# Four graph layers in one kernel: the attention layer's low halves accumulated into the high halves' columns

## The reference, cut to what matters

```python
x = (meta_x @ W).reshape(N, HEADS, DIM)              # HEADS = 4, DIM = 64
a_src = jnp.sum(x * att_src, axis=-1)
a_dst = jnp.sum(x * att_dst, axis=-1)
logits = jax.nn.leaky_relu(a_src[src] + a_dst[dst], 0.2)
ex = jnp.exp(logits - seg_max[dst])
alpha = ex / (seg_sum[dst] + 1e-16)                  # sums over the edges into dst
out = segment_sum(x[src] * alpha, dst).mean(heads) + bias
```

## Time and profile before

| | |
|---|---|
| runs | 1197.7, 1198.29, 1210.78 us, median 1198.29 us |
| profiled execution | 1197.28 us, span 1195.4 us |
| mean granted clock of PE | 0.968 |
| attention, first mask product to last | 772.57 to 1187.08 us |
| after the last product | 8.32 us |

### The profile page before, as it was taken

The page is one execution under the profiler, slowest core; times in us unless marked ns, Lnnn a source line. Parts: engine busy times, 40 slices in busy tenths (PEclk is TensorE's granted clock), DMA queues, the critical chain, the costliest instruction groups (busy, mean ns, idle before and its releaser), DMA issues.

```text
span 1195.4 us, 38826 instructions
## 1 busy us (share of the span) xinstructions
PE 1082.5 (91%) x15999; PEld 997.2 (83%) x15999; DVE 863.9 (72%) x2311; ACT 628.7 (53%) x1172; POOL 59.6 (5%) x106
## 2 busy tenths in 40 slices
PE   4877777779999999999998999599999999999997
PEld 3766666669999999999973999489989988998996
DVE  5999999975444444444562544789999999999997
ACT  2777777730000000000111402579989999998997
POOL 1000000001111111111000011000000000000000
PEclk7899999989999999999999799699999999999999
DMA  5555555510000000000000000000000000000010
GB/s 80 69 78 77 72 74 73 71 39 3 2 3 2 3 2 3 2 2 3 2 2 1 2 2 2 15 12 13 24 12 24 13 24 13 24 13 20 16 29 14
DMA packets 135931, 28.04 MB, mean 23 GB/s; under 512 B 132609, under 2 KB 133093, under 8 KB 135778
## 3 DMA queue, kind: packets, MB, share of 16 engines
q1 hardware_dynamic: 132816, 25.25, 12.9%
q10 hardware_dynamic: 2962, 0.58, 0.3%
HBM read 24.97 MB, written 0.85 MB: 22 GB/s over the span
## 4 chain that ended last, share of the span: by engine, by line
PE 63%; DVE 12%; ACT 3%; issue 2%; ACTq 0%; POOL 0%; DVEq 0%
PE bank L2018 33%; PE bank L2141 13%; PE bank L2137 6%; DVE Mr L1587 4%; PE bank L1955 3%; PE bank L2207 2%; PE bank L1947 2%; ACT Mr L966 1%; DVE F L1487 1%; PE bank L1982 1%; PE bank L1939 1%; ACT F L907 1%; PE bank L2040 1%; DVE Mr L1597 1%; DVE FN L1489 0%
## 5 line engine op out<-in xcount | busy, mean ns | idle before, releaser
L2018 PE MATMUL bank<-GH,C 128*128 128x128 f16 x7100 | 397.7, 219 | 0.0
L2018 PEld LDWEIGHTS bank<-GH,C 128*128 128x128 f16 x7100 | 396.9, 98 | 0.1
L2141 PE MATMUL bank<-F,Mr 128*128 128x260 f16 (+1 forms) x2538 | 321.2, 261 | 10.0 <-DVE Mr L1587 8.7
L2141 PEld LDWEIGHTS bank<-F,Mr 128*128 128x128 f16 x2538 | 213.2, 98 | 33.7 <-DVE Mr L1587 11.0
L1587 DVE TENSOR_TENSOR Mr<-Mr,C 128x640 f16<-128x640 f16 x461 | 207.6, 485 | 25.4 <-ACT Mr L966 24.3
L814 ACT ACTIVATE plo<-bank 128x256 f32<-128x256 f32 (+1 forms) x84 | 30.1, 360 | 364.3 <-PE bank L2018 346.0
L2137 PE MATMUL bank<-FN,C 128*128 128x130 f16 x1945 | 187.3, 220 | 0.0
L1234 DVE TENSOR_TENSOR S<-bank,plo 128x256 f32<-128x256 f32 (+1 forms) x84 | 33.2, 395 | 212.9 <-ACT plo L814 212.8
L1810 PE MATMUL bank<-ohk,ohp 128*128 128x100 f16 (+3 forms) x1452 | 115.9, 216 | 69.6 <-ACT C L756 35.1
L966 ACT ACTIVATE Mr<-cold,eaT 128x640 f16<-128x640 f32 x231 | 172.4, 819 | 8.1 <-PE bank L2141 7.7
L966 ACT ACTIVATE Mr<-eaT 128x640 f16<-128x640 f32 x230 | 171.7, 818 | 7.3 <-PE bank L2141 7.0
(11 more groups left out here) (271 smaller groups left out, 984.4 us busy)
## 6 DMA issues: line engine op xcount, KB each, us to landing
raw<-in_edges_dram SPq DMA_DIRECT2D x237, 68.0 KB, 2.5
cold<-minus_dram SPq DMA_DIRECT2D x10, 320.0 KB, 3.3
eaT<-minus_dram SPq DMA_DIRECT2D x9, 320.0 KB, 3.5
xs<-in_x_dram SPq DMA_DIRECT2D x1, 800.0 KB, 4.4
out_dram<-xs SPq DMA_DIRECT2D x4, 160.0 KB
raw<-in_edges_dram ACTq DMA_DIRECT2D x5, 68.0 KB, 3.2
dsts<-in_dst_dram SPq DMA_DIRECT2D x1, 240.0 KB
dsts<-in_dst_dram ACTq DMA_DIRECT2D x1, 180.0 KB
```

Source lines behind the costliest of these rows:

```text
L2018: last = pe.matmul(bank[:, b, jj * 2 * D:(jj + 1) * 2 * D], C[:, t, (t0 + jj) * P:(t0 + jj + 1) * P], GH[:, par, t, :], start=t == 0 and j ...
L2141: return pe.matmul(bank[:, k, a_:z_], Mr[:, mi % RB, j * P:(j + 1) * P], F[:, t, a_:z_], start=start, stop=t == T - 1)
```

## The change

- `FS` = 16: both copies of the features are scaled by 16 in place of 2048 (`E2`), the high part is the plain float16 rounding, the low part the unscaled difference (a TENSOR_TENSOR subtraction in place of a SCALAR_TENSOR_TENSOR at L1487).
- High and low parts go into the same columns of PSUM. `plain`, `masked` and the `Nr` products each become two products with the same weights, one of the high part and one of the low part, accumulated into the same columns: 260 columns become 2 x 130 (two runs of 65 each), 130 become 2 x 65.
- What is taken out of PSUM is therefore 65 columns a copy in place of 130 (`take`, `evicted`, `tile_in`), `r1` is half as wide, and the addition of the low parts (L1502, L1609) is gone. `q` is gone, `r1` takes its place.
- Bounds: `WIDEST` 12 in place of 16; a second maximum over the weights with the bound `HEAVIEST` = 3.5 on the squared column norm; two small operations on DVE for it in the first hop.
- SP waits for its store of `minus_row` before it looks at the flag, not behind it.

```diff
@@ attention, ACT
-    act.activation(pairs_of(t0)[:, :, 0, :], Vx[gi % 2]..., ACT.Copy, scale=1.0 / LO).then_inc(s_fhi, 1)
+    act.activation(pairs_of(t0)[:, :, 0, :], Vx[gi % 2]..., ACT.Copy).then_inc(s_fhi, 1)
...
-    act.activation(r1[:, j], bank[:, BANKS[b][j], 0:2 * S1], ACT.Identity, scale=ex[:, 1, h, t:t + 1]).then_inc(s_c2, 1)
+    act.activation(r1[:, j], bank[:, BANKS[b][j], 0:S1], ACT.Identity, scale=ex[:, 1, h, t:t + 1]).then_inc(s_c2, 1)
@@ weights(3), DVE
-    c.add(v.tensor_reduce(wmax[:], bank[0:1, 7, 0:GS + H], AX, ALU.max))
+    c.add(v.tensor_reduce(wmax[:, 0:1], bank[0:1, 7, 0:GS + H], AX, ALU.max))
+    c.add(v.tensor_reduce(wmax[:, 1:2], bank[0:1, 7, 0:H * D], AX, ALU.max))
+    c.here()
+    c.add(v.scalar_tensor_tensor(wmax[:, 0:1], wmax[:, 1:2], 900.0 / HEAVIEST, wmax[:, 0:1], ALU.mult, ALU.max))
@@ low_f, evicted, post, DVE
-    c.add(v.scalar_tensor_tensor(pairs_of(t0)[:, :, 1, :], pairs_of(t0)[:, :, 0, :], -LO, Vx[gi % 2]..., ALU.mult, ALU.add))
+    c.add(v.tensor_tensor(pairs_of(t0)[:, :, 1, :], Vx[gi % 2]..., pairs_of(t0)[:, :, 0, :], ALU.subtract))
...
-    v.scalar_tensor_tensor(r1[:, j], bank[:, BANKS[b][j], 2 * S1:4 * S1], ex[:, 3, h, t:t + 1], r1[:, j], ALU.mult, ALU.add)
+    v.scalar_tensor_tensor(r1[:, j], bank[:, BANKS[b][j], S1:2 * S1], ex[:, 3, h, t:t + 1], r1[:, j], ALU.mult, ALU.add)
...
-    c.add(v.scalar_tensor_tensor(q, r1[:, :, S1:2 * S1], 1.0 / LO, r1[:, :, 0:S1], ALU.mult, ALU.add))
-    c.here()
-    c.add(v.tensor_scalar(rd[:], q[:, :, D], 1e-16 * XS, float(H), ALU.add, ALU.mult))
+    c.add(v.tensor_scalar(rd[:], r1[:, :, D], 1e-16 * XS * FS, float(H), ALU.add, ALU.mult))
@@ plain, masked, complement products, PE
-    pe.matmul(bank[:, k, 2 * S1:4 * S1], C[:, t, t_ * P:(t_ + 1) * P], FN[:, t, :], start=start, stop=False)
+    for l in range(2):
+        pe.matmul(bank[:, k, S1:2 * S1], C[:, t, t_ * P:(t_ + 1) * P], FN[:, t, l * S1:(l + 1) * S1], start=start and l == 0, stop=False)
...
-    return pe.matmul(bank[:, k, a_:z_], Mr[:, mi % RB, j * P:(j + 1) * P], F[:, t, a_:z_], start=start, stop=t == T - 1)
+    into = bank[:, k, a_ // 2:z_ // 2].rearrange("p (e c) -> p e c", c=S1)
+    for l in range(2):
+        last = pe.matmul(into, Mr[:, mi % RB, j * P:(j + 1) * P], F[:, t, a_:z_].rearrange("p (e l c) -> p e l c", l=2, c=S1)[:, :, l, :], ...)
+    return last
```

More of the change, by code:

```diff
@@ L63, in gnn_kernel @@
     XS = 256.0
+    FS = 16.0
     S1 = D + 1
@@ L93, in gnn_kernel @@
     GS = H * D + H
-    WIDEST = 16.0
+    WIDEST = 12.0
+    HEAVIEST = 3.5
     STEEP = 2.0 ** 40
@@ L906, in high_f @@
                     act.wait_ge(s_Mu, unit(h - 1, NG - 1, t0 + NT - 1) + 1)
-                act.activation(pairs_of(t0)[:, :, 0, :], Vx[gi % 2].rearrange("p t e c -> p (t e) c"), ACT.Copy, scale=1.0 / LO).then_inc(s_fhi, 1)
+                act.activation(pairs_of(t0)[:, :, 0, :], Vx[gi % 2].rearrange("p t e c -> p (t e) c"), ACT.Copy).then_inc(s_fhi, 1)
             def copy_nad():
@@ L971, in _ @@
                     act.wait_ge(s_Mu, unit(H - 1, NG - 1, T - LATE) + j + 1)
-                    act.activation(r1[:, j], bank[:, BANKS[NG - 1][j], 0:2 * S1], ACT.Identity, scale=ex[:, 1, H - 1, t:t + 1]).then_inc(s_c2, 1)
+                    act.activation(r1[:, j], bank[:, BANKS[NG - 1][j], 0:S1], ACT.Identity, scale=ex[:, 1, H - 1, t:t + 1]).then_inc(s_c2, 1)
                 for part_, (a_, z_) in enumerate(((0, FRONT), (FRONT, NT))):
@@ L1460, in _ @@
             v.wait_ge(s_exp, 1)
-            c.add(v.tensor_scalar(E2[:, 0], E2[:, 0], LO, None, ALU.mult))
-            c.add(v.tensor_scalar(E2[:, 1], E2[:, 1], -LO, None, ALU.mult))
+            c.add(v.tensor_scalar(E2[:, 0], E2[:, 0], FS, None, ALU.mult))
+            c.add(v.tensor_scalar(E2[:, 1], E2[:, 1], -FS, None, ALU.mult))
             c.here()
@@ L2135, in plain @@
                 def plain(k, t_, t, start):
-                    pe.matmul(bank[:, k, 2 * S1:4 * S1], C[:, t, t_ * P:(t_ + 1) * P], FN[:, t, :], start=start, stop=False)
+                    for l in range(2):
+                        pe.matmul(bank[:, k, S1:2 * S1], C[:, t, t_ * P:(t_ + 1) * P], FN[:, t, l * S1:(l + 1) * S1], start=start and l == 0, stop=False)
                 def masked(k, mi, j, t, a_, z_, start):
-                    return pe.matmul(bank[:, k, a_:z_], Mr[:, mi % RB, j * P:(j + 1) * P], F[:, t, a_:z_], start=start, stop=t == T - 1)
+                    into = bank[:, k, a_ // 2:z_ // 2].rearrange("p (e c) -> p e c", c=S1)
+                    for l in range(2):
+                        last = pe.matmul(into, Mr[:, mi % RB, j * P:(j + 1) * P], F[:, t, a_:z_].rearrange("p (e l c) -> p e l c", l=2, c=S1)[:, :, l, :], start=start and l == 0, stop=t == T - 1 and l == 1)
+                    return last
                 xw(0, 1)
@@ L2206, in _ @@
                                 for j in range(NT):
-                                    last = pe.matmul(bank[:, BANKS[b][j], 2 * S1:4 * S1], Nr[ni % RN][:, j * P:(j + 1) * P], F[:, t - 1, 2 * S1:4 * S1], start=False, stop=False)
+                                    for l in range(2):
+                                        last = pe.matmul(bank[:, BANKS[b][j], S1:2 * S1], Nr[ni % RN][:, j * P:(j + 1) * P], F[:, t - 1, (2 + l) * S1:(3 + l) * S1], start=False, stop=False)
                                 last.then_inc(s_Nu, 1)
```

25 lines of the change are left out of this document (11 added, 14 removed).

## The result

The changed kernel takes 1214.01 us (median of 18 runs) against 1198.10 us before (18 runs): a ratio of 1.0132 [1.0110, 1.0154]. It is slower by 15.9 us where +8.7 was forecast: on the forecast side, inside the 2% that count as no change and inside the wide range of 1194 to 1228, and at the upper edge of the forecast's own range, 1198 to 1214. The profiled execution took 1212.48 us with a span of 1210.5, that is +15.20 on the one before.

What follows compares the result with a forecast made beforehand. It took PE to bound attention, with DVE and ACT close behind. PE's added 15.4 us, partly hidden, summed to +9.5, less 0.8 in the tail: +8.7, forecast 1207 us; own range 1198 to 1214, wide range 1194 to 1228.

Steps and rivals of the forecast that it cites:

- PE bounds the middle blocks: Attention's nine middle blocks: PE has no idle time, so its added 0.75 us a block lands in full, 6.8 us.
- The pair of 130: Mask products of 260 columns on PE, cut in two: 115 ns against 111, +4 ns each, 7.6 us over 1907.
- The pair of 65: Products of 130 columns on PE, cut in two: 60 ns against 57.5, +2.5 each, 7.8 us over 3131.
- two things not shown by a row: PE's rates: odd start of second halves and masked's two runs with a gap; PE's price bounded by 3.5 and 35 us.
- Where the price lands: Attention's 20 blocks: PE's added time less what idle time and DVE's relief of 0.83 us a block absorb, +9.5 us.
- the last head: Its four later blocks: DVE paces and is relieved until PE paces again, +0.3 us each, 1.2 in all.
- block 0: Three blocks 0 of later heads: PE idles 0.8 us for DVE, which is relieved by 0.83, so 0.
- block 4: Three blocks 4: PE's 0.6 us of idle time comes late, half counted, +0.4 us each, 1.2 in all.
- The tail: After the last product: L1609's first call (0.36 us), its smaller second and narrower last evictions save 0.8 us.
- Relief wins: Rival, blocks 4 and 0: doubled products cost only their low bound, PE's idle time is given back; 1194 us, chance 0.14.
- Odd width: Rival, PE: products of 65 columns and of two runs cost what L1810's do, +27.7 us, 1226; chance 0.14.
- Supply as a floor: Rival, PE's instruction supply: short products don't come in long streams; at a 56 ns floor about 1350 us, chance 0.07.

Runs made afterwards that it cites:

- e3: Changed kernel with the old evictions of 130 columns and L1502's addition put back, doubled products kept, added results unused: 1215.62 us, ratio 1.0138.
- e4: Kernel before with its products unchanged, only the high halves' columns taken out and no addition of low parts: 1191.87 us, ratio 0.9931.
- e9: Kernel before with only the mask's products of 260 columns cut into two of 130, one run each: 1201.76 us, ratio 1.0026.
- e7: Changed kernel with only FN's halves stored 144 bytes apart, each beginning at a multiple of 16 bytes: 1210.45 us, ratio 1.0104.
- e6: Kernel before with only its tables for splitting work among PE, DVE and ACT retuned: 1186.29 us, ratio 0.9903.
- e1: Changed kernel with the order of high and low half swapped, so fewer products begin right behind the one ahead: 1210.16 us, ratio 1.0125.
- e2: Changed kernel with every half stored 66 columns apart, so that each begins at an even element: 1214.73 us, ratio 1.0136.
- e8: Kernel before with only plain's products cut into two of 65, each into columns of its own: 1203.18 us, ratio 1.0029.

## Why the prediction was right in kind and short in size

- **PE bounds the middle blocks: right.** They grew by 1.28 us with PE busy throughout, and taking DVE's and ACT's relief away (e3) or giving it alone (e4) moves them by at most 0.01 and 0.05 us.
- **The pair of 130: right.** +4 ns forecast, 57.64 x 2 - 110.95 = +4.3 measured; two runs with a gap cost no more on the mean than halves in one run each (e9).
- **The pair of 65: the step that failed.** "60 against 57.5, +2.5 ns": measured 31.41 x 2 - 57.37 = +5.45 for `plain`, +5.8 for the mask's, +5.5 for the complement's. The 30 ns came from one piece of ten products, and it was right for that row: behind the first step of a burst, 39 ns, the 64-column products of the trace before take 29.6 on the mean. But the row was not the nearest in pattern. It is 64 columns wide, and a 65th is 0.41 ns (a column, by (110.95 - 57.04) / 130). And the two parts of the features that its products read (`whl`, L2103) lie apart, where the halves of `FN` and `F` follow one another; this placement is not among the "two things not shown by a row". Of the missing 1.41 ns, 1.06 is placement, since `plain` with its halves apart takes 30.35 (e7); the other 0.35 is the width and the step of 35, which these runs don't separate. The price of placement stood in the trace before: in L2137's rows of 17 in the middle blocks, the products of 130 columns that begin in the 16 bytes in which the one ahead ended take 59.4 ns, the others 56.4. Over 3131 products it makes 17 us in place of 7.8, and PE's whole added time 1907 x 4.3 + 17 = 25 us in place of 15.4, inside the bounds of 3.5 and 35 that were kept for it.
- **Where the price lands: right for the last head once the price is right; block 0 in part by luck; the reason for block 4 was wrong.** In the last head the forecast of 0.3 leaves 0.45 of the price to DVE's pacing; 1.28 less the 0.48 of e4 is 0.80, and 0.83 was measured. Block 0: 0 forecast, -0.06 measured. But by the forecast's own rule the true price, 1.28, less the relief of 0.83 would have left some 0.45. The block had more room than the idle 0.8 that its stretch shows: with as many products and other tables it takes 21.15 us, PE busy throughout (e6), 1.1 less than before. Relief alone gives 0.80 there (e4), and doubled products alone cost 0.34 (e3). Blocks 4 took 0.59 us; the forecast's rule (price less half of the idle 0.6) would by the true price give nearly 1.0. Nor was it the relief that helped: it moves block 4 by 0.00 us alone (e4) and by 0.01 when taken back (e3, 22.28). The doubled products ran into PE's idle time there, which fell from 0.62 to 0.09 us. The first block's +0.40 is not resolved: among kernels that share its products (e1, e2, e3, e7) it lasts 28.06 to 28.48 us.
- **The tail: mis-sized.** -0.8 forecast, -0.25 measured. Over the traces the tail lasts 7.97 to 8.18 us with the narrow takeout (the change, e1, e2, e7) and 8.22 to 8.30 with the old one (before, e3, e8, e9), so 0.1 to 0.3 is what the change is worth there. I counted L1609's calls in full as lying on the last chain; which of the tail's steps took up the difference was not tried.
- **The rivals.** "Relief wins" fell: its low price did not hold, though the relief that it counted, 5.5 us, is there when nothing is added (e4, 6.3 us, in blocks 0 and the last head, not in blocks 4). Of "Odd width" the odd start fell (e2); an even width was not tried, but products of 65 columns that begin apart mostly take 29 ns (e7), as those of 64 do. Its price of +6.7 for a pair was nearer to the measured 5.5 than mine, for another reason than it gave. The 45.8 ns that the forecast took for 110 columns have no row beside them, but the trace before shows the rate: in the hops products of 512 columns (L1955) start every 216 ns and those of 128 every 56, so a column is (216 - 56) / 384 = 0.417 ns, 2.4 of them a ns. Supply as a floor fell: 511 products in a block of 20.16 us are one every 39 ns, and the two thirds of them that are 65 columns wide come at 31.

## What to carry to other kernels

A product that is cut in two pays twice for what is not columns, here 4 to 6 ns a cut, of which some 2 ns in a pair of 65 are placement, which storing `plain`'s halves apart gave back (e7). On PE, which has no idle time in the middle blocks, this was added in full, +1.28 us a block, and relief of the others bought at most 0.05 us there (e4). Read a rate from hundreds of starts, product by product, correct it for the width, and see whether the row that it comes from lies in memory as yours will: a half nanosecond on 6262 products is 3 us. When a change leaves slack on other engines, retune the split of work before judging it, and give the kernel before the same retuning: here it had room of its own, and came out ahead.

## What the runs showed of the hardware

- Products of 65 columns with their own weight loads come at 30.4 (e7) to 31.7 ns (e8) on the mean of the stage, not at the 29 of their fastest steps, at a granted clock of 1.00.
- A 65-column product whose features begin in the 16 bytes in which those of the one ahead ended takes 33 ns to the next start in place of 29 (after, e2), and one of 130 columns 59.4 in place of 56.4 (before). Where it begins right behind them, but at a multiple of 16 bytes, it takes 29.1 (after, 36 steps in the middle blocks' rows of 34) and 55.9 (before, 18 steps in their rows of 17).
- With that gone a step of 35 ns comes up every fifth product or so (e1, e7). In the bursts of ten 64-column products only the first step is long (39 ns). Its cause is open.
- Products of 130 columns in two runs of 65 with a gap take 57.6 ns each (after); in one run 55.8 where they begin apart from the one ahead and 59.5 where they begin behind it (e9).
